# SyncE's issue order in each turn of a fused attention and FFN kernel: x's transpose, the store of y and the refill of x change places

## The chip, the cores and the metric

The kernel runs on one core of one Trainium2 chip. The metric is the device time in microseconds; the time before is the median of three runs. Beside the runs there is one profiled execution, whose trace is read here. TensorE is PE, VectorE is DVE, ScalarE is ACT, GpSimd is POOL, and SyncE, which only issues DMAs here, is SP.

## The reference

The input x has 2 sequences of 2048 tokens with 256 features. Everything is computed from its layer norm:

```
xn = layernorm(x)
s  = attention(xn)          # 16 heads of 16, q and k of unit length, window of 128 tokens, ALiBi, softmax, then Wo
g  = silu(ffn(xn))          # h = silu(xq @ gate) * (xq @ up), 704 hidden; then h @ down
                            # x, h and the weights are rounded blockwise (16) to FP4 before each product
out = x + s * g
```

## The kernel before, in words

The 4096 tokens are 32 tiles of 128. The work is one software pipeline: in each turn every engine runs a piece of several tiles, in an order that is written out by hand for each engine. All waits between engines are semaphores. The steady part is a loop over t = 8 to 30 on SP (the other engines' loops run over t = 4 to 30); the turns before and after are written out.

Matmuls need their left operand with the contraction on the partitions, so three things are turned by DMA, from SBUF to SBUF, each issued by SP:

- `stack_transpose(t)` (L1845): q and k of a tile, from `qk_stack` to `qk_slots`. The scores of the tile need it.
- `ah_transpose(g)` (L1870): the attention output and the rounded h of tile g, 15 blocks of 128x128 fp16, from `ah_stack` to `ahT`. `wo_mm(g)` (L574) and `down_mm(g)` (L560) on PE need it.
- `x_transpose(u)` (L1859): 8 blocks of 128x128, the normalised x of tile u and the rounded x of tile u-2, from `x_stack` to `xT`. `qk_mm`, `v_mm`, `gate_mm` and `up_mm` (all through the helper at L372) need it.

SP issues two plain DMAs a turn as well: `store(i)` (L1886) writes the finished y of tile i to the output, and `refill(i)` (L1892, the turns t = 8 to 23) loads tile i+16 of x into the ring slot that tile i has left. Three y buffers go round: `gated(i)` on DVE (L928) waits until the store of tile i-3 has landed. The refilled tile is first read by `ln_stats` on DVE (L735).

One ring of dependences goes round once a turn. When `ah_transpose(g)` has landed, PE runs `wo_mm(g)`, scores, `up_mm`, the rest of the weighing of the values (L584), scores again and `down_mm(g)`; ACT takes the silu of it (L1335); `gated(g)` (L928) multiplies; POOL adds x in `add_x(g)` (L1575), and behind it in its own order stands `lo_att(g+1)` (L1569), the last piece of `ah_stack` for the next tile. That releases `ah_transpose(g+1)`. The same queues hold the rest of the work.

Here SP's turn t stands beside PE's turn t+2: `ah_transpose(t-2)` is used at once, `x_transpose(t+3)` first by `qk_mm(t+3)` at the end of the same PE turn.

Of the kernel before, what the change touches and what calls it, by code (L numbers as in the profile page):

```python
# [81 lines left out]
def build(nc, x_d, wproj_d, wg_d, wu_d, wd_d, keyfac_d, ident_d, mask_d, out_d):  # L82
    ctx = ExitStack()
    with ctx:
# [245 lines left out]
        def exists(t):  # L330
            return 0 <= t < TILES

        def turn_parts(u):

            return slice(0 if exists(u) else 1, 2 if exists(u - LAG) else 1)
# [1502 lines left out]
        def sync_program(e):  # L1838
            def stack_transpose(t):
                e.wait_ge(s_lo_qk, t + 1)  # L1840
                if t >= 1:
                    e.wait_ge(l_qkT, 16 * t)
                if t >= Q_SLOTS - 1:
                    e.wait_ge(s_scores[3], t - Q_SLOTS + 2)
                e.dma_start_transpose(qk_slots[:, t % Q_SLOTS],  # L1845
                                      qk_stack[t % S_BUFS][:].rearrange("p h s d -> p (h s d)")).then_inc(l_qkT, 16)

            def x_transpose(u):
                if exists(u):
                    e.wait_ge(s_lo_xn, u + 1)  # L1850
                if exists(u - LAG):
                    e.wait_ge(s_hi_qx, u - LAG + 1)
                    e.wait_ge(s_lo_qx, u - LAG + 1)
                if exists(u - 2):
                    e.wait_ge(s_v_mm, u - 1)
                if exists(u - 2 - LAG):
                    e.wait_ge(s_up_mm, u - 1 - LAG)
                parts = turn_parts(u)
                e.dma_start_transpose(xT_all[u % 2][:, parts.start * 2 * KT:parts.stop * 2 * KT, :],  # L1859
                                      x_stack[u % 2][:, parts].rearrange("p a b d -> p (a b d)")  # L1860
                                      ).then_inc(l_xT[u % 2], 16)

            def ah_transpose(g):
                e.wait_ge(s_hi_h, g + 1)
                e.wait_ge(s_lo_h, g + 1)
                e.wait_ge(s_lo_att, g + 1)
                if g >= 2:
                    e.wait_ge(s_down_mm, g - 1)
                    e.wait_ge(s_wo_mm, g - 1)
                e.dma_start_transpose(ahT[g % 2][:], ah_stack[g % 2]).then_inc(l_ahT[g % 2], 16)  # L1870
# [10 lines left out]
            def store(i):  # L1881
                if i < LAST:
                    e.wait_ge(s_y, i + 1)
                else:
                    e.wait_ge(s_y_last, 1)
                e.dma_start(out_d[i * P:(i + 1) * P, :], y[i % Y_BUFS][:]).then_inc(stored[i % Y_BUFS], 16)  # L1886

            def refill(i):

                e.wait_ge(s_y, i + 1)  # L1890
                e.wait_ge(l_qkT, 16 * (i + 6))
                e.dma_start(x_all[:, i % X_RING, :], x_d[(i + X_RING) * P:(i + X_RING + 1) * P, :]  # L1892
                            ).then_inc(l_refill[i], 16)
# [60 lines left out]
            for t in range(8, 31):  # L1954
                stack_transpose(t + 1)
                ah_transpose(t - 2)
                if exists(t - 8) and exists(t - 8 + X_RING):
                    refill(t - 8)
                store(t - 5)
                x_transpose(t + 3)  # L1960
            store(TILES - 6)
            ah_transpose(TILES - 3)
            ah_transpose(TILES - 2)
# [9 lines left out]
        with nc.Block() as block:  # L1973
            @block.tensor
            def _(e): tensor_program(e)

            @block.vector
            def _(e): vector_program(e)

            @block.scalar  # L1980
            def _(e): scalar_program(e)

            @block.gpsimd
            def _(e): gpsimd_program(e)

            @block.sync
            def _(e): sync_program(e)
# [27 lines left out]
```

## Time and profile before

| | us |
|---|---|
| median of 3 runs | 535.02 |
| lowest, highest | 531.51, 536.55 |
| the profiled execution, its own time | 538.59 |
| its span, first to last instruction | 536.8 |
| PE busy | 447.4 (83%) |
| DVE busy | 414.8 (77%) |
| POOL busy | 376.2 (70%) |
| ACT busy | 364.9 (68%) |

The span is the part that the trace shows; 1.8 us of the execution's time lie around it. The profiled execution is 3.6 us above the median of the three runs. The mean granted clock of PE is 0.977 of full speed over the span.

### The profile page before, as it was taken

What the parts mean: (1) busy time and instruction counts of PE and PEld (TensorE: products, weight loads), DVE (VectorE), ACT (ScalarE), POOL (GpSimd) and SP (SyncE); (2) the same over time, 40 slices, a digit from 0 to 9 for tenths busy, and PEclk for the clock granted to TensorE, in tenths of its full rate; (3) what the DMA queues carried; (4) which work ended last, traced back from release to release, by engine and by line L of the source; (5) the groups of instructions that cost most, each with busy time, mean ns of one, the idle gap of its engine ahead of it and who ended that gap; (6) DMA issues with size and microseconds to landing.
All of it is one profiled execution on the core that took longest, in us unless ns stands there. A gap on an engine that the chain in (4) does not pass through costs nothing.

```text
span 536.8 us, 21323 instructions
## 1 busy us (share of the span) xinstructions
PE 447.4 (83%) x8612; PEld 309.0 (58%) x8612; DVE 414.8 (77%) x776; ACT 364.9 (68%) x559; POOL 376.2 (70%) x854
## 2 busy tenths in 40 slices
PE   0138887998998889999998899899999998999975
PEld 0025554665665556666666466566666666667653
DVE  3897988886886777888887688868888887876572
ACT  3544988785775676777776677667777777777640
POOL 3864468875777756778878767757788878766262
PEclk9999999998998898999999899989999999999998
DMA  8202127553464753466656666735566654565443
GB/s 296 80 11 60 40 61 146 98 94 66 113 113 78 118 99 74 107 114 118 117 96 101 116 117 116 113 73 107 108 115 117 108 98 79 107 109 100 107 72 90
DMA packets 175010, 54.40 MB, mean 101 GB/s; under 512 B 164224, under 2 KB 174272, under 8 KB 174912
## 3 DMA queue, kind: packets, MB, share of 16 engines
q1 hardware_dynamic: 174480, 52.90, 51.9%
q8 instruction: 68, 1.11, 0.9%
q14 instruction: 30, 0.25, 0.2%
q10 hardware_dynamic: 432, 0.13, 0.1%
HBM read 7.54 MB, written 4.19 MB: 22 GB/s over the span
## 4 chain that ended last, share of the span: by engine, by line
PE 44%; DMA 23%; DVE 10%; POOL 8%; issue 6%; ACT 3%; SPq 2%; DVEq 0%; POOLq 0%
DMA ahT<-ah_stack 23%; PE up L372 12%; PE gt L560 10%; PE bank_b L584 7%; PE gt L574 5%; POOL y L1575 3%; POOL ah_stack L1569 3%; PE scores L517 3%; DVE y L928 2%; PE bank_b L378 2%; ACT ffn_gate L1335 2%; PE gt L372 1%; PE scores L541 1%; PE bank_q L372 1%; SPq L1859 1%
## 5 line engine op out<-in xcount | busy, mean ns | idle before, releaser
L1322 ACT ACTIVATE probs<-scores 128x768 f32<-128x768 f32 (+1 forms) x101 | 80.3, 795 | 57.0 <-PE scores L541 51.3
L584 PE MATMUL bank_b<-probs,vals 64*32 64x64 f32 (+1 forms) x3904 | 74.8, 220 | 13.8 <-DVE vals L905 13.7
L584 PEld LDWEIGHTS bank_b<-probs,vals 64*32 64x32 f32 (+1 forms) x3904 | 60.6, 108 | 31.2 <-DVE vals L905 16.9
L372 PE MATMUL up<-wgu_hi,xT 128*128 128x352 f16 x248 | 66.0, 334 | 0.0
L372 PE MATMUL gt<-wgu_hi,xT 128*128 128x352 f16 x256 | 62.4, 312 | 1.2 <-DVE y L928 1.2
L372 PE MATMUL bank_q<-wproj_hi,xT 128*128 128x512 f16 x128 | 45.2, 394 | 16.9 <-DMA xT<-x_stack 9.8
L787 DVE SCALAR_TENSOR_TENSOR up<-up,h_gain,gate 128x704 f32<-128x704 f32 x31 | 29.7, 958 | 30.6 <-PE up L372 29.2
L1575 POOL TENSOR_TENSOR y<-y,x_all 128x256 f32<-128x256 f32 x31 | 23.1, 746 | 40.5 <-DVE y L928 40.5
L560 PE MATMUL gt<-wdn_lo,ahT 128*128 128x256 f16 x192 | 46.4, 277 | 0.0
L574 PE MATMUL gt<-wo_hi,ahT 128*128 128x256 f16 x120 | 26.6, 288 | 21.7 <-DMA ahT<-ah_stack 21.6
L1556 POOL TENSOR_TENSOR ah_stack<-h_grid,h_coarse 128x704 f16<-128x704 bf16 x31 | 42.5, 1370 | 2.5 <-DVE h_grid L824 2.5
L560 PE MATMUL gt<-wdn_hi,ahT 128*128 128x256 f16 x160 | 39.4, 278 | 5.4 <-DMA ahT<-ah_stack 5.4
L767 DVE TENSOR_TENSOR x_ring<-x_ring,x_rscale 128x256 f32<-128x256 f32 x32 | 43.9, 1371 | 0.0
L1564 POOL TENSOR_TENSOR ah_stack<-h_grid,h_fine 128x704 f16<-128x704 bf16 x31 | 42.9, 1383 | 1.3 <-DVE h_grid L824 1.3
L1185 ACT ACTIVATE pv_t<-bank_b 128x512 f32<-128x512 f32 x31 | 18.5, 597 | 34.3 <-PE bank_b L584 34.3
L372 PE MATMUL up<-wgu_lo,xT 128*128 128x352 f16 x124 | 41.4, 334 | 0.0
L1322 ACT ACT_TABLE_LOAD x31 | 39.8, 1283 | 0.5
L372 PE MATMUL gt<-wgu_lo,xT 128*128 128x352 f16 x128 | 39.9, 312 | 0.0
L1185 ACT ACTIVATE qk_stack<-bank_q 128x512 f16<-128x512 f32 x64 | 34.8, 599 | 7.0 <-DVE bank_q L884 6.8
L372 PEld LDWEIGHTS gt<-wgu_hi,xT 128*128 128x128 f16 x256 | 24.9, 97 | 24.6 <-issue 12.6
L1335 ACT ACT_TABLE_LOAD x29 | 37.2, 1283 | 0.5
L1329 ACT ACTIVATE gate<-gt,unpower 128x704 f32<-128x704 f32 x31 | 26.3, 847 | 16.0 <-PE gt L372 16.0
(231 smaller groups left out, 1370.2 us busy)
## 6 DMA issues: line engine op xcount, KB each, us to landing
out<-y SPq DMA_DIRECT2D x32, 128.0 KB, 3.3
x_all<-x SPq DMA_DIRECT2D x20, 128.0 KB, 3.9
x_all<-x SPq DMA_DIRECT2D x3, 512.0 KB, 4.4
x_all<-wproj SPq DMA_DIRECT2D x1, 768.0 KB, 7.4
dn_raw<-wd SPq DMA_DIRECT2D x1, 704.0 KB, 9.1
probs<-wg SPq DMA_DIRECT2D x1, 640.0 KB, 5.6
probs<-wu SPq DMA_DIRECT2D x1, 640.0 KB, 8.0
xT<-x_stack SPq DMA_TRANSPOSE x34, 4.0
```

The source lines that it names most:

```text
L372: done = e.matmul(out, lhs[i][:, kt, :], rhs[j][:, kt, lo:hi], start=n == 0, stop=n == len(terms) - 1)
L560: done = e.matmul(bank_c[:, 0:D], aT[:, slot, :], w, start=n == 0, stop=n == len(terms) - 1)
L574: done = e.matmul(wo_out(i), ahT[i % 2][:, (ATT_HI, ATT_LO)[i_] + k, :], wo[j_][:, k, :], start=n == 0, stop=n == len(terms) - 1)
L584: done = e.matmul(pv_bank(i)[32 * n:32 * n + 32, grp * P + q:grp * P + q + HB], va, pr, start=first and grp == 0, stop=last and grp == 3)
L767: e.tensor_tensor(blocks(xq[t % 2]), blocks(xn[t % XN_BUFS]), per_block(x_rscale[:]), ALU.mult).then_inc(s_x_step[NORM], 1)
L787: e.scalar_tensor_tensor(up_of(t), up_of(t), h_gain[:], gate_of(t), ALU.mult, ALU.mult).then_inc(s_h, 1)
L1185: return e.activation(out, src, ACT.Copy)
L1322: e.activation(probs[j % P_BUFS][:, grp, :, window(j)].rearrange("p (b e) w -> p b e w", b=2), score_banks(j, grp)[:, :, :, window(j)], AC ...
L1335: e.activation(ffn_gate[g % FG_BUFS][:], bank_c[:, 0:D], ACT.Silu, scale=down_inv[:]).then_inc(s_fgate, 1)
L1556: e.tensor_tensor(blocks(ah_stack[t % 2][:, H_HI:H_HI + FF]), blocks(grid_of(t)), per_block(h_coarse[t % 2][:]), ALU.mult).then_inc(s_hi_h, 1)
L1564: e.tensor_tensor(blocks(ah_stack[t % 2][:, H_LO:H_LO + FF]), blocks(grid_of(t)), per_block(h_fine[t % 2][:]), ALU.mult).then_inc(s_lo_h, 1)
L1575: e.tensor_tensor(yb[:], yb[:], x_all[:, i % X_RING, :], ALU.add).then_inc(s_y, 1)
```

## The change

In the 23 turns of SP's loop, the two transposes of the turn still come first; then x's transpose, the store and the refill follow in this order, where it was refill, store, x's transpose. Nothing else differs: the waits in front of each DMA, the buffers and all other engines' programs are the same.

```
             for t in range(8, 31):
                 stack_transpose(t + 1)
                 ah_transpose(t - 2)
+                x_transpose(t + 3)
+                store(t - 5)
                 if exists(t - 8) and exists(t - 8 + X_RING):
                     refill(t - 8)
-                store(t - 5)
-                x_transpose(t + 3)
```

On SP, turns t = 11 and 12 of the loop, with a refill, stand so before (`ahT1<-ah_stack` is `ah_transpose(9)`, `xT0` is `x_transpose(14)`, `out<-y0` is `store(6)`, `x_all<-x` is `refill(3)`):

```order
L1845 DMA_TRANSPOSE qk_slots<-qk_stack0 128x16x128
L1870 DMA_TRANSPOSE ahT1<-ah_stack 128x15x128
L1892 DMA x_all<-x 128x256
L1886 DMA out<-y0 128x256
L1859 DMA_TRANSPOSE xT0<-x_stack0 128x8x128
L1845 DMA_TRANSPOSE qk_slots<-qk_stack1 128x16x128
L1870 DMA_TRANSPOSE ahT0<-ah_stack 128x15x128
```

The same two turns after the change:

```order
L1845 DMA_TRANSPOSE qk_slots<-qk_stack0 128x16x128
L1870 DMA_TRANSPOSE ahT1<-ah_stack 128x15x128
L1859 DMA_TRANSPOSE xT0<-x_stack0 128x8x128
L1886 DMA out<-y0 128x256
L1892 DMA x_all<-x 128x256
L1845 DMA_TRANSPOSE qk_slots<-qk_stack1 128x16x128
L1870 DMA_TRANSPOSE ahT0<-ah_stack 128x15x128
```

x's transpose moved up two places, to stand right behind that of h; the refill moved down two, and the store moved behind x's transpose.

On SP, the last turn of the loop (t = 30) and the first issues behind it, before (`out<-y1` is `store(25)`, `xT1` is `x_transpose(33)`):

```order
L1845 DMA_TRANSPOSE qk_slots<-qk_stack1 128x16x128
L1870 DMA_TRANSPOSE ahT0<-ah_stack 128x15x128
L1886 DMA out<-y1 128x256
L1859 DMA_TRANSPOSE xT1<-x_stack1 128x4x128
L1886 DMA out<-y2 128x256
L1870 DMA_TRANSPOSE ahT1<-ah_stack 128x15x128
```

And after:

```order
L1845 DMA_TRANSPOSE qk_slots<-qk_stack1 128x16x128
L1870 DMA_TRANSPOSE ahT0<-ah_stack 128x15x128
L1859 DMA_TRANSPOSE xT1<-x_stack1 128x4x128
L1886 DMA out<-y1 128x256
L1886 DMA out<-y2 128x256
L1870 DMA_TRANSPOSE ahT1<-ah_stack 128x15x128
```

Here `store(25)` now stands behind `x_transpose(33)`.

## Rows read from the trace of the kernel before

**Rows 1.** The chain that ended last, by line.

```profile
DMA ahT<-ah_stack 23%; PE up L372 12%; PE gt L560 10%; PE bank_b L584 7%; PE gt L574 5%; POOL y L1575 3%; POOL ah_stack L1569 3%; PE scores L517 3%; DVE y L928 2%; PE bank_b L378 2%; ACT ffn_gate L1335 2%; PE gt L372 1%; PE scores L541 1%; PE bank_q L372 1%; SPq L1859 1%
```

**Rows 2.** The chain in order of time, one turn (start us, us, what).

```profile
226.67 4.12 DMA ahT<-ah_stack
...
238.55 0.49 DVE y L928
...
240.69 4.12 DMA ahT<-ah_stack
```

**Rows 3.** The chain again: h's transpose in other turns, issue to landing.

```profile
148.22 4.12 DMA ahT<-ah_stack
162.25 5.48 DMA ahT<-ah_stack
...
283.08 5.38 DMA ahT<-ah_stack
...
401.80 4.10 DMA ahT<-ah_stack
```

**Rows 4.** Stretches: us, busy per engine, PEclk, DMA share, GB/s.

```profile
162.25:167.70 5.45, 3.25 (x113) 2.27 (x111) 3.87 (x10) 3.64 (x4) 4.16 (x16) 0.99 0.90 122
162.25:179.11 16.86, 14.58 (x273) 9.79 (x272) 11.73 (x23) 10.64 (x16) 11.26 (x26) 0.90 0.48 86
167.70:171.10 3.40, 3.32 (x31) 1.95 (x32) 1.84 (x2) 1.10 (x2) 3.40 (x4) 0.51 0.25 70
283.08:298.27 15.19, 12.99 (x257) 9.08 (x256) 11.74 (x23) 9.79 (x16) 11.22 (x26) 1.00 0.60 105
```

**Rows 5.** SP's issues in time, turns of 162.25 and 226.67.

```profile
165.85 1.38 SPq L1886 DMA_DIRECT2D out<-y  x1
...
228.33 1.15 SPq L1892 DMA_DIRECT2D x_all<-x  x1
...
230.14 1.43 SPq L1859 DMA_TRANSPOSE xT<-x_stack  x1
236.87 1.60 SPq L1845 DMA_TRANSPOSE qk_slots<-qk_stack  x1
```

**Rows 6.** SP's own waits, 179 to 500 us: total, times, longest.

```profile
SPq L1845 <- DVE qk_stack L893: 128.6, 22, 8.0
SPq L1868 <- POOL ah_stack L1569: 44.8, 22, 2.1
```

**Rows 7.** DMA issues, KB, us to landing: 226.6:231, then 148.2:153.

```profile
xT<-x_stack SPq DMA_TRANSPOSE x1, 4.7
...
xT<-x_stack SPq DMA_TRANSPOSE x1, 5.3
```

**Rows 8.** Landing times of all stores, from the view by source line.

```profile
DMA to landing us min/median/max: 1.7/3.3/5.0
```

**Rows 9.** First users of that turn's xT and of its refilled slot.

```profile
237.77 0.38 PE L372 MATMUL bank_q<-wproj_hi,xT 128*128 128x512 f16 x1
...
258.81 0.37 DVE L735 BATCH_NORM_STATS2 stats<-x_all 128x6 f32<-128x256 f32 x1
```

**Rows 10.** All waits of PE between 175 and 500 us.

```profile
PE gt L574 <- DMA ahT<-ah_stack: 16.3, 21, 2.1
PE bank_b L584 <- DVE vals L905: 11.1, 21, 0.6
PE gt L372 <- DVE y L928: 1.2, 1, 1.2
```

**Rows 11.** DMA queues, 0.05 us at 165.80, then 405.35: packets, MB, share.

```profile
q8 instruction: 1, 0.02, 134.2%
...
q8 instruction: 1, 0.02, 203.4%
```

**Rows 12.** The last turn of SP's loop, and DVE's write of tile 28.

```profile
504.07 1.20 SPq L1859 DMA_TRANSPOSE xT<-x_stack  x1
...
511.82 0.48 DVE L928 SCALAR_TENSOR_TENSOR y<-gt,out_inv,ffn_gate 128x256 f32<-128x256 f32 x1 [0.79 <-ACT ffn_gate L1335]
```

More of the change, by code:

```diff
@@ L1956, in sync_program @@
                 ah_transpose(t - 2)
+                x_transpose(t + 3)
+                store(t - 5)
                 if exists(t - 8) and exists(t - 8 + X_RING):
                     refill(t - 8)
-                store(t - 5)
-                x_transpose(t + 3)
             store(TILES - 6)
```

## The prediction

> **What bounds the kernel now.** I read the chain that ended last first: the reader is to see there which work sets the end, not which engine is busiest. Its largest line is a DMA, the transpose of h, with 23% of the span [rows 1]. Followed through one turn, the chain is a closed ring: 4.12 us from the issue of h's transpose to its landing, then PE's work of the turn, the silu, DVE's product at 238.55, POOL's add, POOL's last piece of `ah_stack`, and the next issue 14.02 us after the first [rows 2]. Nothing else that SP issues is in this ring. The waits of PE say the same from the other side: between 175 and 500 us it waited for three things only, 16.3 us for `ahT`, 11.1 us for the scaled values and 1.2 us for a y, and never for `xT` [rows 10].
>
> Then I compared turns, since they are not equal. The landing of h's transpose has two levels: 4.1 us (turns issued at 148.22, 226.67, 401.80) and 5.4 to 5.5 us (162.25, 283.08) [rows 2, 3]. The turn of 226.67 takes 14.02 us, that of 283.08 takes 15.19, that of 162.25 takes 16.86. In the last one PE was busy for only 3.25 of the first 5.45 us, waiting for `ahT` at their end, and then the granted clock is 0.51 from 167.70 to 171.10, the lower of TensorE's two levels (1.2 against 2.4 GHz); in the turn of 283.08 it stays at 1.00 [rows 4]. So a landing that is some 1.3 us late (5.48 less 4.12 is 1.36) costs 1.2 us of turn where the clock stays, and 2.84 us (16.86 less 14.02) where it falls.
>
> What makes a landing late is seen in the DMA queues: 3.55 to 3.60 us behind the issue of 162.25, just as the transpose is finishing, a single 16 KB instruction packet starts. Its time is 1.342 x 0.05 us x 16 = 1.07 us on one of the 16 DMA engines [rows 11], and the landing comes 5.48 us after the issue, behind the packet's end. The ring's one DMA can be held up by what else stands in the DMA engines, and the change alters just that.
>
> **The change part by part.** No DMA is added or removed, and no wait is: the conditions stand in front of the same DMAs. I take the turn of 226.67 as the pattern.
>
> *x's transpose, earlier.* Its waits are for pieces of `x_stack` which in POOL's order stand ahead of the piece that releases h's transpose, and for products that PE made a turn earlier. From 179 to 500 us SP waits only in front of the transposes of q and k (22 times) and of h (22 times), never at L1859 [rows 6]. So it goes out at once behind h's transpose: at 228.33, where the refill was, instead of 230.14, 1.81 us earlier [rows 5]. It takes 4.7 us to land in this turn, and 5.3 in the one of 148.22, where x does follow h directly [rows 7]; so it lands at 233.0 to 233.6 instead of 234.8. Its first user starts at 237.77 [rows 9]. It had 2.9 us to spare and has 4.1 to 4.8 now: worth 0.
>
> *The store, behind x's transpose.* In the turn of 162.25 the order h, x, store stands already: the store goes out 3.60 us after h's transpose [rows 3, 5]. So here it goes out at 230.27. Landing takes 1.7 to 5.0 us over all 32 stores [rows 8]; with the worst, 235.3. Who waits for it is `gated` of the tile three further on, at 238.55, which is in the ring [rows 2]. 3.3 us remain even then: cost 0. The cover is thin enough to name: if it were gone, every microsecond of lateness would go into the turn.
>
> *The refill, last.* The store's issue takes up to 1.38 us [rows 5], so the refill goes out at about 231.8 instead of 228.33. The tile is first read at 258.81 [rows 9]: 27 us for one load of 128 KB, cost 0.
>
> *What stands behind on SP.* The refill's issue (1.15 us) ends by 233.0; the next transpose of q and k is issued at 236.87, when its data are ready [rows 5]. 3.9 us to spare: 0.
>
> *The last turn.* There x's transpose did wait, until 504.07. The store of tile 25 stood ahead of it and will stand behind, at about 505.3 (504.07 and 1.20 for the issue). With the worst landing of 5.0 us it is out by 510.3; `gated(28)` writes the same buffer at 511.82 [rows 8, 12]. 1.5 us remain at worst, 3.2 us at the median landing of 3.3 us. Cost 0, but this is the nearest edge.
>
> *h's own transpose, with another transpose right behind it.* This is the only term that touches the ring. 256 KB of plain copies followed it in the DMA engines, and 256 KB of transposing ones will. Two turns have that order already. In the turn of 148.22 the landing is 4.12 us, the same as in the turn of 226.67 with copies behind [rows 2, 3]. In the turn of 162.25 it is 5.48 us with an instruction packet in the way [rows 3, 11], where the turn of 283.08, with copies behind, shows 5.38. From below: the quiet landings lie between 4.10 and 4.12, so a gain is 23 x 0.02 = 0.5 us at most. From above: 1.36 us in each turn where a packet starts as the transpose's own data end (the first rival). I take 0, since the quiet turn of 148.22 is the nearest row for a quiet turn and the 0.1 us between 5.48 and 5.38 is all that a late one shows.
>
> The Trainium skill, DMA: Bandwidth & Descriptors, section Queues, rings and completion order, says that a DMA engine takes its descriptors in ring order, and that the completion increment lands only after all earlier writes of that engine, those of its other queues too. By the first half, work put behind h's transpose can't hold it; by the second, an instruction packet ahead of the increment can. The turns of 148.22 (4.12 us) and 162.25 (5.48 us) agree, one with each half. By this page alone the sum is 0 too.
>
> The sum is six times 0, so 0 us against the profiled execution's 538.6 us (a span of 536.8 and 1.8 around it). That execution lies 3.6 us above the median of the three runs, about what one or two late turns are worth, so the forecast is the median: 535.0 us.
>
> **The rivals.** *Slower: x's transpose holds h's completion.* Mechanism: with transposes behind it in each DMA engine, the end of h's transpose stays open to an instruction packet for longer. For it: in the turn of 162.25, x behind, a packet that starts 3.55 to 3.60 us after the issue makes the landing 5.48 us; in the turn of 401.80, refill behind, one that starts in the same place (405.35 to 405.40) and lasts longer, 2.034 x 0.05 x 16 = 1.63 us, leaves it at 4.10 us [rows 3, 11]. Against it: this is one pair, and which DMA engine takes the packet isn't seen; if it had finished its share, the order behind doesn't matter. Price: six turns of the loop have a packet between 3.5 us after the issue and the landing, that of 401.80 among them, and land early now. If all became late, 6 x 1.2 = 7 us with the clock kept and 6 x 2.84 = 17 us with it lost; half of each gives 12 us: 547 us. It passes 1% from the third such turn on.
>
> *Slower: a store late.* In the last turn the store would have to land 1.5 us later than the worst of all; that costs 1 to 2 us, once: 537 us, within 1%. In the plain turns it would have to be 3.3 us worse than the worst, and would then cost 23 us for each microsecond; no row comes near.
>
> *Faster: some late landings go away.* If the copies draw out a late landing, or if the packets fall into other places once SP's order differs, one to three of the trace's seven late turns could become quiet. Three of the dear ones give 3 x 2.84 = 8.5 us: 526.5 us. Against it: PE's program is unchanged, so its instruction packets come at the same places of it, and the late turn of 162.25 has no refill behind it at all.
>
> *The moved transpose is needed earlier somewhere.* That would show as a wait of PE for `xT`; rows 10 have none, so this gives 535.0 again and has no chance of its own.
>
> **How the numbers follow.** No change, the late store of the last turn included: 0.75, at 535.0 us, with the scatter of the three runs, 531.5 to 536.6, around it. The held completion: 0.12, at 547 us. Enough late turns fewer to pass 1%: 0.10, 526.5 to 529.6 us. An unforeseen cost beyond 1%: 0.03. A difference of 1%, 5.4 us, is about what a measurement of this kernel can tell from no change. So faster 0.10, same 0.75, slower 0.15. The range takes in two dear late turns fewer, 535.0 - 5.7 = 529.3, and on the other side most of the held completion's cheap half, three dear turns more, 535.0 + 8.5 = 543.5.
>
> **What the changed profile would show.** Right: `xT` issued 1.7 us after `ahT` and the store 3.6 us after it, no wait of PE for `xT`, quiet turns of 14.02 us with landings of 4.1 us, the loop's last store at 505 us and no wait for it at `gated(28)`. Wrong: more than nine turns with landings over 5 us, quiet turns other than 14.0 us, or DVE waiting for a store at L928. The forecast fails if the number of late turns with a lowered clock moves by more than two; it is the one quantity here that the rows of one execution can't pin down.

## The result, and the profile after

The changed kernel takes 561.54 us (median of 4 runs, 558.81 to 568.1) against 533.69 us before (4 runs, 531.51 to 536.55). The ratio is 1.050, with a 95% interval of 1.041 to 1.059: 5% slower. The profiled execution took 558.81 us, with a span of 557.0 us; that of before had 536.8. So the traces are 20.2 us apart, and it is this that is accounted for below; the medians of the runs are 27.9 us apart, and no trace shows the rest. The time of one kernel scatters by up to a few per cent from execution to execution, so each ratio here rests on the faster runs (it is not the quotient of the medians), and from an execution that was one of its kernel's slower ones (those of e3, e5, e9, e13 and e14) only the landings of single turns are used.

The chain that ended last, by line, of the changed kernel [compare rows 1]:

```profile
DMA ahT<-ah_stack 25%; PE up L372 12%; PE gt L560 9%; PE bank_b L584 6%; PE gt L574 5%; POOL y L1575 3%; POOL ah_stack L1569 3%; PE scores L517 3%; DVE y L928 2%; PE bank_b L378 2%; ACT ffn_gate L1335 2%; PE scores L541 1%; PE bank_q L372 1%; PE gt L372 1%; PE scores L538 1%
```

It is the same chain, and the transpose of h has grown from 23% of 536.8 us to 25% of 557.0. The longest waits of PE from 175 to 520 us (us in total, times, longest) name nothing new either [compare rows 10]:

```profile
PE gt L574 <- DMA ahT<-ah_stack: 26.5, 21, 2.5
PE bank_b L584 <- DVE vals L905: 11.1, 21, 0.6
PE gt L372 <- DVE y L928: 0.7, 1, 0.7
```

No wait for `xT`, and none for a store: in the same 21 waits PE stood 10.2 us longer for `ahT`. SP's issues in one turn of the changed kernel (start us, us) [compare rows 5]:

```profile
240.23 1.56 SPq L1870 DMA_TRANSPOSE ahT<-ah_stack  x1
241.97 1.81 SPq L1859 DMA_TRANSPOSE xT<-x_stack  x1
243.83 1.61 SPq L1886 DMA_DIRECT2D out<-y  x1
245.55 0.37 SPq L1892 DMA_DIRECT2D x_all<-x  x1
```

x's transpose goes out 1.74 us after h's and the store 3.60 us after h's, as computed. The turns are where the time is; stretches of the changed kernel, with the columns of rows 4:

```profile
226.14:240.23 14.09, 13.12 (x273) 9.18 (x272) 11.74 (x23) 10.64 (x16) 11.20 (x26) 1.00 0.53 112
240.23:258.90 18.67, 16.04 (x273) 10.42 (x272) 11.85 (x23) 10.64 (x16) 11.29 (x26) 0.82 0.50 85
258.90:274.35 15.45, 13.12 (x273) 9.18 (x272) 11.74 (x23) 10.65 (x16) 11.24 (x26) 1.00 0.60 102
274.35:293.23 18.88, 15.86 (x273) 10.23 (x272) 11.76 (x23) 10.64 (x16) 11.28 (x26) 0.82 0.53 84
338.45:355.69 17.24, 14.69 (x273) 9.77 (x272) 11.75 (x23) 10.65 (x16) 11.29 (x26) 0.90 0.50 92
415.34:431.11 15.77, 13.12 (x273) 9.18 (x272) 11.74 (x23) 10.65 (x16) 11.24 (x26) 1.00 0.61 100
445.21:463.75 18.54, 15.98 (x273) 10.39 (x272) 11.86 (x23) 10.65 (x16) 11.28 (x26) 0.82 0.46 79
```

The first is a quiet turn, 14.09 us against 14.02. The six behind it are those of t = 12, 13, 14, 18, 23 and 25 in SP's loop. In the kernel before, the same turns took 14.03, 14.05, 14.31, 14.02, 14.02 and 14.23 us (the distances from one issue of h's transpose to the next). The differences are 4.64, 1.40, 4.57, 3.22, 1.75 and 4.31 us, 19.9 us together. The other turns from t = 8 to 28 add 0.4 us between them. What is left cancels and is no part of this account: the last two turns of the loop are 2.4 us longer than before, the part ahead of the loop is 0.8 us shorter and the part behind it 1.7 us shorter. Nearly all of the 2.4 us is the turn of t = 30 (first after, then before), whose landing took 6.64 us against 4.50, with a packet 4.64 us behind the issue; x's transpose was issued 4.29 us behind there, so this turn is not explained by what follows:

```profile
519.25:533.96 14.71, 12.70 (x301) 8.96 (x303) 6.06 (x10) 8.73 (x12) 4.32 (x6) 1.00 0.49 88
```

```profile
499.27:512.09 12.82, 12.82 (x305) 9.29 (x306) 6.14 (x11) 9.16 (x12) 4.62 (x7) 1.00 0.46 101
```

Inside the turn of 240.23, from the chain in order of time:

```profile
240.23 5.82 DMA ahT<-ah_stack
...
246.09 1.46 PE gt L574 x6
...
248.23 3.64 PE up L372 x12
...
258.90 5.53 DMA ahT<-ah_stack
```

The landing is late (5.82 us against 4.12 in a quiet turn [rows 2]), and the PE work behind it is slow: the 12 matmuls of `up_mm` stand with 3.64 us on the chain. The granted clock in the 5.27 us from the issue, in which PE was busy for 3.24, and in the next 4 us, in which h landed (at 246.05):

```profile
240.23:245.50 5.27, 3.24 (x113) 2.26 (x111) 3.67 (x10) 3.64 (x4) 3.98 (x16) 1.00 1.05 121
245.50:249.50 4.00, 3.40 (x31) 2.00 (x32) 2.03 (x2) 1.18 (x2) 3.92 (x5) 0.52 0.35 100
```

0.52 is the lower of the clock's two levels (1.2 GHz), after PE had stood idle for `ahT`.

And what stands beside each late landing, in the DMA queues (packets, MB, share of 16 engines). In the changed kernel, in the 0.1 or 0.05 us from 243.70, 278.00 and 418.95, that is 3.5 to 3.7 us behind the issues of 240.23, 274.35 and 415.34:

```profile
q8 instruction: 1, 0.02, 83.2%
...
q8 instruction: 1, 0.02, 204.4%
...
q8 instruction: 1, 0.02, 165.9%
```

Each is one 16 KB instruction packet, of 1.33, 1.64 and 1.33 us. All six turns have one between 3.5 and 3.9 us after h's issue. Six turns of the kernel before had one in that place or just behind it too, and landed in 4.1 to 4.4 us; that of 401.80 is the one of which the prediction has the rows [rows 3, 11]. Five of them are the same turns of the loop (t = 13, 14, 18, 23, 25). The sixth changed: at t = 22 the packet now comes 4.43 us after the issue, behind the landing, and at t = 12 it comes at 3.51 where it came at 4.75.

What the packet does to the traffic can be seen. These are the GB/s of all DMA traffic in 40 slices of 0.15 us, first from 240.2, the late turn of 240.23; then, in the kernel e1 of the next section, which has a copy between h and x, from 249.6, where h is issued at 249.65 and a packet starts 3.60 us later; then, in the kernel before, from 283.0 (h issued at 283.08, packet at 2.60 us):

```profile
GB/s 0 0 0 0 0 0 0 5 143 217 218 215 210 213 200 222 217 218 218 218 208 183 207 306 220 200 196 164 36 0 0 0 5 9 10 9 10 10 207 290
```

```profile
GB/s 0 0 0 0 0 0 0 0 108 224 215 212 217 205 208 220 220 215 220 217 215 184 215 277 439 328 69 0 119 213 203 196 113 27 7 7 14 15 19 20
```

```profile
GB/s 0 55 0 0 0 0 0 0 75 212 222 215 208 207 201 208 224 323 200 152 26 0 0 0 7 9 10 9 10 166 294 285 359 389 376 273 362 279 276 246
```

The packet is a single one, yet the transposing traffic of the whole core falls from some 200 GB/s to 10 or less, and comes back. In the turn of 240.23 x's data follow h's without a hole, this pause runs from 4.3 to 5.7 us behind h's issue, and h lands at 5.82. In all six late turns h lands 0.1 to 0.2 us after the traffic comes back. In e1 x's data start only at 4.15 us, h has landed at 4.12, and the pause (from 5.0 us) holds x alone. In the turn of 283.08 it holds h's own data, from 3.1 to 4.3 us.

### The profile page after: what moved, and what is told of

It reads as the page before. It is cut to its first block, busy times and chain, and to the rows that moved or that the text cites. A ratio compares the mean times of both kernels' runs of the same rounds, so it can differ in the third digit from the quotient of the medians.

```text
span 557.0 us, 21323 instructions
## 1 busy us (share of the span) xinstructions
PE 457.7 (82%) x8612; PEld 313.2 (56%) x8612; DVE 415.9 (75%) x776; ACT 364.9 (66%) x559; POOL 377.0 (68%) x854
## 4 chain that ended last, share of the span: by engine, by line
PE 41%; DMA 25%; POOL 10%; DVE 9%; issue 6%; ACT 2%; SPq 1%; DVEq 0%; POOLq 0%
DMA ahT<-ah_stack 25%; PE up L372 12%; PE gt L560 9%; PE bank_b L584 6%; PE gt L574 5%; POOL y L1575 3%; POOL ah_stack L1569 3%; PE scores L517 3%; DVE y L928 2%; PE bank_b L378 2%; ACT ffn_gate L1335 2%; PE scores L541 1%; PE bank_q L372 1%; PE gt L372 1%; PE scores L538 1%
## 5 line engine op out<-in xcount | busy, mean ns | idle before, releaser
L584 PE MATMUL bank_b<-probs,vals 64*32 64x64 f32 (+1 forms) x3904 | 76.0, 222 | 14.0 <-DVE vals L905 13.7
L372 PE MATMUL up<-wgu_hi,xT 128*128 128x352 f16 x248 | 70.4, 352 | 0.0
L574 PE MATMUL gt<-wo_hi,ahT 128*128 128x256 f16 x120 | 29.3, 308 | 32.7 <-DMA ahT<-ah_stack 32.7
L372 PE MATMUL up<-wgu_lo,xT 128*128 128x352 f16 x124 | 43.7, 352 | 0.0
L517 PE MATMUL scores<-hidden_keys,neg 64*64 64x256 f16 x404 | 32.1, 308 | 6.4 <-ACT probs L1322 2.8
```

The costliest lines, as they stand in the source:

```text
L372: done = e.matmul(out, lhs[i][:, kt, :], rhs[j][:, kt, lo:hi], start=n == 0, stop=n == len(terms) - 1)
L517: e.matmul(banks[c * HB:c * HB + HB, b, :, w:w + P], neg16[r, r], hide, start=True, stop=False)
L574: done = e.matmul(wo_out(i), ahT[i % 2][:, (ATT_HI, ATT_LO)[i_] + k, :], wo[j_][:, k, :], start=n == 0, stop=n == len(terms) - 1)
L584: done = e.matmul(pv_bank(i)[32 * n:32 * n + 32, grp * P + q:grp * P + q + HB], va, pr, start=first and grp == 0, stop=last and grp == 3)
```

## The experiments

Every kernel below is the changed one with the lines shown, unless said otherwise; each ratio is to the kernel before on the same chip. In the texts, `h` stands for `ah_transpose(t - 2)`, `x` for `x_transpose(t + 3)`; the `if` around the refill is left out of the cuts of code.

**e1, a copy between.**

```
                 ah_transpose(t - 2)
-                x_transpose(t + 3)
                 store(t - 5)
+                x_transpose(t + 3)
                 refill
```

> Order h, store, x, refill: one plain copy of 128 KB now stands between the transpose of h and that of x. Theory A (a transpose directly behind h's in the DMA engines leaves h's landing open to an instruction packet that starts 3.5 to 3.9 us after the issue): time like before, 533 to 537 us, and landings over 5 us only where a packet starts between 1.8 and 3.5 us after the issue. Theory B (what costs is that the refill stands last, or that x's transpose is moved up at all): like the changed kernel, 555 to 562 us. Theory C (a matter of how much transposing follows closely; one copy is too thin a shield): between, 540 to 552 us.

534.54 us, ratio 0.996 (0.992 to 1.000). Theory A holds so far; B and C fall. Seven turns have a packet at 3.5 to 4.0 us, and none of them is late. Two of them, from the chain of e1:

```profile
249.65 4.12 DMA ahT<-ah_stack
263.69 4.11 DMA ahT<-ah_stack
```

and the packets in the 0.1 and 0.05 us from 253.20 and 267.30:

```profile
q8 instruction: 1, 0.02, 82.9%
...
q8 instruction: 1, 0.02, 199.9%
```

The second packet is about as long as the one of 278.00 above (1.60 us against 1.64), comes at the same point, and delays nothing.

**e2, both copies ahead of h.** `store` and `refill` moved ahead of `ah_transpose`, x directly behind it.

> Order store, refill, h, x: both copies go out ahead of the transpose of h, when their data are long ready, and x's transpose stands alone behind h's. Theory A (transpose directly behind transpose): slow like the changed kernel, 553 to 562 us, with late landings for packets at 3.5 to 3.9 us. Theory B (the copies' late place costs): like before, 533 to 537 us. If the copies' issues push h's own issue back, every turn grows and no quiet turn of 14.0 to 14.1 us is left.

550.71 us, ratio 1.025 (1.017 to 1.032). Slow, and with the place of the copies out of the question; but less slow than A said. Its trace shows why: only two turns of the loop have a packet at 3.45 to 4.0 us, not six. Both are late. One is (chain, then the queues in the 0.1 us from 438.1):

```profile
434.69 5.60 DMA ahT<-ah_stack
```

```profile
q8 instruction: 1, 0.02, 76.5%
```

One more (416.01) is late at a packet 4.27 us behind. So the number of such meetings, which I had taken as fixed, moves with the order, and the time with it.

**e3, nothing behind h.**

```
                 ah_transpose(t - 2)
+                e.wait_ge(*ahT_landed(t - 2))
                 x_transpose(t + 3)
```

> The changed order h, x, store, refill, but SyncE waits for h's landing before it issues x: nothing at all stands behind h in the DMA engines. Theory A: not slower than before, 529 to 536 us, though x, store and refill all come 2.5 us later than in the changed kernel. Theory B (x or the copies in a bad place relative to the rest of the turn): 555 us or more. If the copies that follow h in the kernel before also cost something, this one is faster than before, below 530 us.

536.81 us, ratio 1.000 (0.994 to 1.005). Theory A holds, B falls again. All three DMAs come later than in the changed kernel and cost nothing, so their lateness was never the matter. It is not faster than before either: plain copies behind h cost nothing. In the loop eight turns have a packet at 3.5 to 3.9 us; seven land in 4.1 us, one (432.05) in 5.95, with nothing behind it at all. In that one two last packets of the transpose start late, between 436.7 and 437.2, about when the instruction packet (3.86 us behind the issue, 1.04 us long) ends:

```profile
q1 hardware_dynamic: 2, 0.00, 0.6%
```

So a packet in this place can still catch the tail of h itself; it did so once in the eight turns.

**e4, x ahead of h.** The order q and k, x, h, store, refill.

> Order q and k, x, h, store, refill: x's transpose goes ahead of h's, in the time in which SyncE waits for h's data, and only copies stand behind h. Theory A: like before, 531 to 537 us, as long as x is out of the DMA engines when h starts (x is ready 2.8 us before h's issue). If x's transpose still runs then, h's landing grows to 4.3 to 4.7 us in every turn and the time goes to 540 to 550 us. Theory B (x moved up costs): 555 us or more.

544.64 us, ratio 1.013 (1.004 to 1.023): neither of the two forecasts. The landings are like before (4.1 to 4.6 us in quiet turns, six late ones among t = 8 to 28). The last turn isn't; SP's issues there in e4:

```profile
499.02 1.59 SPq L1845 DMA_TRANSPOSE qk_slots<-qk_stack  x1
505.64 1.19 SPq L1859 DMA_TRANSPOSE xT<-x_stack  x1
507.00 1.63 SPq L1870 DMA_TRANSPOSE ahT<-ah_stack  x1
```

x's data come late in this one turn, and h, ready, queues behind it: 8.0 us behind the transpose of q and k, where it was 1.75 us in the kernel before.

**e5, a small transpose directly behind h, in the kernel before.**

```
                 ah_transpose(t - 2)
+                spare_transpose(t - 8)    # one 128x128 block of a constant into a spare buffer
                 refill
                 store(t - 5)
                 x_transpose(t + 3)
```

> The order of the kernel before (h, refill, store, x), with one small DMA more directly behind h in each of the 23 turns: a transpose of a single 128x128 block of a constant into a spare buffer that nobody reads. If the kind alone matters (any transposing DMA directly behind h opens its landing to an instruction packet at 3.5 to 3.9 us): five or six late turns more, 548 to 560 us. If it is the volume of transposing work behind h (x has 8 such blocks, some 1.2 us of DMA time, this one an eighth): like before, 533 to 539 us, with a landing of 4.1 us for packets at 3.5 to 3.9 us.

553.73 us, ratio 1.020 (1.014 to 1.027). x stands in its old place, and some two fifths of the loss are back: five of seven turns with a packet at 3.5 to 3.9 us are late. (In the two that are not, the small transpose was issued 1.36 us behind h, in the five 1.6 to 1.7 us; why that matters isn't shown.) Two of them and one that is not, from the chain of e5:

```profile
240.72 5.84 DMA ahT<-ah_stack
259.12 4.18 DMA ahT<-ah_stack
273.21 5.72 DMA ahT<-ah_stack
```

So it takes neither x itself nor its volume.

**e6 and e7, the packets moved.** Both the changed kernel (e6) and the one before (e7) get 128 more TensorE instructions at the start, while PE waits for its inputs:

```
+            e.wait_ge(l_ident, 16)
+            for _ in range(64):
+                transposes(bank_q, [ident[:]])
             tr_bound(0)
```

> The changed kernel, with 64 more transposes of the identity on TensorE before its first work (128 instructions of TensorE, half a 16 KB instruction packet, at a time when it waits for inputs; their result is overwritten). The packets then come half a packet earlier in TensorE's program. If instruction packets make h's landing late: other turns of the loop than the 3rd to 7th are late (the turns that were late for a packet at 3.5 to 3.9 us get none there), each late turn still has a packet between 1.8 and 3.9 us after h's issue, and the time stays 3 to 7% above the equally shifted kernel before. If packets are not the cause: the same turns are late as in the changed kernel.

> The kernel before, with the same 64 transposes of the identity on TensorE at its start. If packets are the cause: late turns only where a packet starts 1.8 to 3.5 us after h's issue, in other places than before; 525 to 545 us. Else the late turns stay at the 1st, 2nd, 7th, 8th, 11th and 18th turn of the loop.

e6: 543.98 us, 1.015 (1.010 to 1.020) of the kernel before. e7: 532.07 us, 0.988 (0.981 to 0.994). Both against the same runs of before, so e6 is 1.5 + 1.2 = 2.7% above e7 (shown only through before; the range for it was 3 to 7%). The late turns have moved: in e6 the turns of the loop with a late landing are the 2nd to 5th, the 15th, the 16th and the 21st; in the changed kernel there were eleven among t = 8 to 28, and the 3rd and 4th were quiet. The 3rd and 4th turn from the chain of e6 and, behind it, of e7:

```profile
206.97 6.02 DMA ahT<-ah_stack
224.47 5.96 DMA ahT<-ah_stack
```

```profile
209.41 4.13 DMA ahT<-ah_stack
223.45 4.11 DMA ahT<-ah_stack
```

Packets in them (0.05 us from 210.55 in e6, 3rd turn; 0.1 us from 226.90 in e7, 4th turn):

```profile
q8 instruction: 1, 0.02, 189.4%
```

```profile
q8 instruction: 1, 0.02, 114.6%
```

1.52 and 1.83 us long, 3.6 and 3.5 us behind the issue. A packet in this place delays h where x's transpose stands behind it, and not where copies do. And the packets have their part in it: 128 instructions that compute nothing change which turns are late.

**e8, the same hole ahead of the loop.** e1, and in the last written-out turn too `store(2)` goes ahead of `x_transpose(10)`.

> Order h, store, x, refill in the loop, as in the kernel with the store between the two transposes, and in the last written-out turn ahead of the loop too (store of tile 2 ahead of x's transpose for tile 10), the one place of the kernel before where x stands directly behind h and the landing is late at a packet at 3.56 us (5.48 us). Theory A: that turn is quiet (4.1 us, 14.0 us long), 2.8 us less than before where its clock fell: 530 to 533 us. If one copy is no shield there: 534 to 537 us.

531.65 us, ratio 0.992 (0.988 to 0.996). Lower than before, but its interval overlaps that of e1 (0.992 to 1.000), so the further gain isn't shown. That turn (162.25 before, 5.48 us [rows 3]) now reads, in the chain of e8:

```profile
163.94 4.13 DMA ahT<-ah_stack
```

But its packet starts only 4.25 us after the issue, behind the landing, so this turn was not put to the test; in e1, with no copy between, the same turn landed in 4.17 us, with a packet at 4.06.

**e9, a small copy between h and x.** A copy of 32 KB of a constant between them, the rest as changed.

> The changed order h, x, store, refill, with a plain copy of 32 KB (a constant, SBUF to a spare buffer) between the transposes of h and of x in each of the 23 turns. If what counts is which kind stands directly behind h in the queue: the small copy is a shield, quiet landings at packets of 3.5 to 3.9 us, 532 to 540 us. If what counts is that a transposing DMA is in the DMA engines before h has landed (the small copy costs only some 0.1 to 0.2 us of them, where a copy of 128 KB took about 0.5): slow like the changed kernel, 550 to 562 us.

538.06 us, ratio 1.006 (1.003 to 1.010): the small copy is enough, within 1%. I first read that as a shield. But SP's issues in e9 show a second difference:

```profile
244.08 1.63 SPq L1872 DMA_TRANSPOSE ahT<-ah_stack  x1
245.76 1.13 SPq L1879 DMA_DIRECT2D spare<-neg  x1
247.07 1.24 SPq L1861 DMA_TRANSPOSE xT<-x_stack  x1
```

The copy's own issue takes 1.13 us, so x goes out 2.99 us after h and not 1.74. The one late landing of e9 at a packet in this place (331.46; the packet at 3.92 us) is in the turn where x went out soonest, 2.85 us after h:

```profile
331.46 5.78 DMA ahT<-ah_stack
```

**e13 and e14, x later, with nothing between.** These tell the shield from the time.

```
                 ah_transpose(t - 2)
+                e.wait_ge(s_vals, min(t + 3, TILES))      # e13
+                e.wait_ge(s_exp[0], t + 2)                # e14
                 x_transpose(t + 3)
```

> The changed order h, x, store, refill; in the loop SyncE also waits, ahead of x's transpose, for DVE's scaled values of the turn, which are ready some 2.4 us after h's issue. x goes out at about 2.5 us instead of 1.7, with nothing between it and h. If the kind of DMA next behind h decides: slow, 550 to 562 us. If x's issue time decides and the limit lies below 2.5 us: 532 to 538 us; if it lies above 2.5 us: slow here and fast in the run with the later wait.

> The same with a wait for ACT's first exponential of the turn, ready some 3.4 us after h's issue, so that x goes out at 3.5 us, where it went out before the change, but with no copy ahead of it in the DMA engines. If the kind of the next DMA decides: slow, 550 to 562 us, with late landings at packets of 3.5 to 3.9 us. If the issue time decides: 530 to 538 us, like before.

e13: 566.97 us, ratio 1.053 (1.041 to 1.065). e14: 537.55 us, 0.998 (0.992 to 1.005). SP issues x's transpose at these times, in e13 and then in e14:

```profile
241.66 1.56 SPq L1870 DMA_TRANSPOSE ahT<-ah_stack  x1
244.07 1.25 SPq L1859 DMA_TRANSPOSE xT<-x_stack  x1
```

```profile
240.63 1.56 SPq L1870 DMA_TRANSPOSE ahT<-ah_stack  x1
244.10 1.79 SPq L1859 DMA_TRANSPOSE xT<-x_stack  x1
```

2.41 us behind h is still too early; 3.47 us is late enough, with no copy between. Those two turns land in (e13, then e14)

```profile
241.66 5.90 DMA ahT<-ah_stack
```

```profile
240.63 4.10 DMA ahT<-ah_stack
```

though both have a packet about 3.6 us behind the issue. So the time decides, and the shield falls: of theory A the part that says "directly behind" was wrong.

**e15, x ahead of h but in the last turn.**

> The order x, h, store, refill in 22 turns, and h, store, x in the last one of the loop, where x's data come 5 us later than h's. If the last turn alone made the order x ahead of h slower (its transpose of h was issued 8.0 us behind that of q and k instead of 1.8): 532 to 537 us, like before. If x ahead of h costs in each turn: 541 us or more.

538.49 us, ratio 1.003 (0.997 to 1.009), 1.5 us above the range. The interval overlaps e4's, so it is the traces that tell: the turns of t = 29 and 30 take 33.3 us in e4 and 25.0 us in e15, as in the kernel before. e4's loss was there.

**e10 to e12, the best order with the packets moved.** e8 with 64, 32 and 96 of the extra transposes.

> The order h, store, x, refill in the loop and store ahead of x in the last written-out turn too, with the 64 extra transposes of the identity at TensorE's start. The shift alone gave 0.988 of before, the order alone 0.992. If they add: 523 to 529 us, with four late turns. If the shift's gain was an accident of one turn: 529 to 534 us.

> The same with 32 extra transposes, a quarter of an instruction packet. The late turns of both kernels come from packets at 1.8 to 3.5 us after h's issue; the quarter shift puts them in yet other turns. If their number is set by the step from turn to turn alone: five to seven late turns, 528 to 536 us. If the places differ in number: anything from three late turns (522 us) to eight (540 us).

> The same with 96 extra transposes, three quarters of an instruction packet: 522 to 540 us by the same reasoning, five to seven late turns expected; packets at 3.5 to 3.9 us leave landings of 4.1 to 4.5 us.

527.79 us, 0.987 (0.981 to 0.993); 531.69 us, 0.994 (0.990 to 0.998); 535.10 us, 1.004 (0.999 to 1.008). e10 has the lowest median of all, but the gains of e7 and e8 don't add (0.992 x 0.988 would be 0.980), and its interval is nearly that of e7 (0.981 to 0.994), whose turn ahead of the loop was quiet too. Both have three late turns among t = 8 to 28, where e8 has six. e11 and e12 have four each, e12 outside its forecast of five to seven. e11's interval overlaps e8's. e12's lies above it, in spite of fewer late turns in the loop; part of that stands ahead of the loop, where its h of t = 6 is issued at 151.50 us against 145.28 in e10. So moving the packets moves late turns about, and the number in the loop alone doesn't give the time.

**All kernels together.** In the profiled execution of each of the 17 kernels, these are 21 turns of the loop (h's issues of t = 8 to 28), sorted by the distance of an instruction packet of 16 KB to h's issue; late means a landing over 4.9 us:

| x's transpose issued | kernels | turns with a packet at 3.45 to 4.05 us | of them late | at 4.05 to 4.35 us | of them late |
|---|---|---|---|---|---|
| 1.4 to 2.5 us after h (in e5 the small one) | after, e2, e5, e6, e13 | 25 | 23 | 12 | 4 |
| 2.85 us or more after h, or ahead of it | before, e1, e3, e4, e7 to e12, e14, e15 | 83 | 2 | 25 | 0 |

The two late ones of the second row are those of e3 (432.05) and e9 (331.46) above. All others of that row that have x behind h have it at 2.95 us or more. A packet at 1.7 to 3.45 us, while h's own data move, makes the landing late in 87 of 87 turns, whatever stands behind.

## Why the prediction was wrong

*What bounds the kernel:* right. The ring through h's transpose is the bound, late landings come from instruction packets, and the clock adds to them.

*x's transpose earlier is worth 0:* right; PE waits for `xT` in neither trace.

*Store and refill late cost 0:* right. They went out where computed in the turns, and e3 sends all of them later still at a ratio of 1.000. In the last turn of the changed kernel the store of tile 25 went out at 525.34 and `gated(28)` started at 533.69, released by ACT: no wait. The margin was larger than the 1.5 us I feared.

*"h's own transpose, with another transpose right behind it: I take 0":* this step failed. I had two turns with that order, 148.22 and 162.25, and took the quiet one for a quiet turn and the late one for an ordinary late one. But the packet of the turn of 162.25 starts 3.55 us after the issue, and the packets that make landings late with copies behind start before 3.45 us (e3 and e9 have one exception each); the right comparison was the one that I put among the rivals, the turn of 401.80. It was not one pair by luck: over all kernels it is 23 of 25 against 2 of 83. The term, put at 0, came out at 19.9 us in six turns. Nor was a quiet turn free: with x behind, the median of the quiet landings (t = 8 to 28) is 4.17 us, where it was 4.12.

*The rule of the Trainium skill:* I let "takes its descriptors in ring order" carry more than it says. It is about the order within one queue of a DMA engine. The other half of the same section of DMA: Bandwidth & Descriptors (the Trainium skill), that the completion increment lands only after all earlier writes of its engine, other queues included, fits the one late turn of e3, where two last packets of h start as the instruction packet ends. No run contradicts it, but it doesn't say that a transpose issued behind makes a landing late at a packet that others pass in 81 of 83 turns, and the runs do.

*The first rival, "x's transpose holds h's completion":* this is what happened, and I gave it 0.12. Its place and its sign were right, its price was too low. The count of six turns was partly luck: five are the turns counted, one dropped out and another came in, as the packets moved against the issues. I took half of the turns at 1.2 us and half at 2.84, 12 us; measured are 1.40 to 4.64 us, 19.9 us in all. A late turn of this kind costs more: the six landings took 5.5 to 6.2 us, not 5.4 to 5.5, and in three of the six the granted clock is 0.50 for 4 us behind the landing. There `up_mm` takes 3.6 us on the chain (1.9 in the quiet turn of 226.14), and 4.3 to 4.6 us are lost where I took 2.84.

*The range* ended at 543.5 us, since it cut the rival off at three dear turns. With a mechanism seen once in the trace and six places waiting for it, it should have reached the rival's own 547 to 552 us. Even that would have missed the measured 561.5 us, of which the traces account for 20 us and not for the rest.

*The signs of being wrong* that the prediction named came: 14 landings over 5 us in the changed kernel's trace, against seven, and eight late turns with a lowered clock, against five.

*The faster rival* has nothing for it: of the seven landings over 5 us none went away.

How the time of x's issue comes in can be read off the traffic. Here it is in the kernel before from 226.6 to 231 us, in 40 slices of 0.11 us (226.67 is h's issue):

```profile
GB/s 0 0 0 0 0 0 0 0 0 0 0 70 207 219 212 228 209 202 212 207 216 216 219 219 223 202 233 212 205 186 212 240 231 186 130 261 317 307 298 307
```

A transpose's data follow its issue by 1.2 us, and x's in e1 did so too (issued at 2.98, moving from 4.15 us). So x issued at 2.4 us is moving before h's usual landing at 4.1, x issued at 2.85 us just so (from 4.0), and x issued at 2.95 us or later is not. A pause that begins then holds the landing of h in the first two cases and x alone in the third. That is worked out from these times; what the runs themselves show is the count in the table.

Left open: why a single packet stops the transposing traffic of all DMA engines, and why h's completion waits for it to come back when h's own data have passed. The limit between 2.85 and 2.95 us rests on one late turn.

## What to carry to other kernels

Where one DMA is in the ring that sets the end, look at what else is in the DMA engines as it finishes, instruction packets included, and put no other transposing DMA there: here 1.7 us of patience on SyncE (e14), or a copy issued in between (e1), undid the whole 5%. When the same transfer lands in 4.1 or 5.5 us, sort the turns by the distance between the issue and whatever meets it before calling one "quiet" and one "late": a pair that differs in just that thing is worth more than the nearest quiet row. And ask of each reordering what happens in the loop's last turn, where the data come in another order (e4 against e15).

## What the runs showed of the hardware

- A 16 KB instruction packet, 0.9 to 1.8 us long, that starts while a transposing DMA of 480 KB moves its data (1.7 to 3.45 us after the issue) made the landing 0.8 to 2.4 us late in 87 of 87 turns. None of the orders tried avoids it. It can be moved: 128 idle TensorE instructions at the start gave a ratio of 0.988.
- With such a packet the transposing traffic of the whole core pauses: from about 200 GB/s to 10 or less for 1.2 to 1.4 us, from some 0.5 to 0.8 us after the packet's start until 0.7 to 0.8 us after its end (turns of 283.08 and 240.23).
- A packet just behind the data (3.45 to 4.05 us after the issue) left 81 of 83 landings in time when copies, nothing, or a transpose issued 2.85 us or more after followed. When a transpose issued 1.4 to 2.5 us after followed, even one of a single 128x128 block, 23 of 25 were late, with landings of 5.4 to 6.2 us.
- In the changed kernel a landing that was 1.4 to 2.1 us late cost 1.4 to 1.8 us of turn with the clock kept, and 3.2 to 4.6 us when the granted clock fell. What decides the clock isn't shown: it fell to 0.50 behind a landing of 5.82 us (240.23) and stayed at 1.00 behind one of 5.85 us (415.34).
